# Pairs inside two neighbouring field groups computed in one burst of 32x64 TensorE tiles instead of two bursts of 64x128 tiles

## The reference, cut to what matters

```
z[b, (i,j)] = sum_e sum_f  e[b,i,e] * W[(i,j),e,f] * e[b,j,f]      # 780 pairs
h = concat(z, dense_ctx)                # 780 + 16
h = relu(h @ W_top1 + b_top1)           # 512
h = relu(h @ W_top2 + b_top2)           # 256
y = h @ W_top3                          # 1
```

## Time and profile before

| | us |
|---|---|
| median of 3 runs (range) | 751.01 (750.84 to 751.55) |
| the profiled execution: its time | 747.58 |
| its span | 745.8 |
| PE busy (share) | 689.6 (92%) |
| DVE busy | 546.2 (73%) |
| POOL busy | 446.0 (60%) |
| ACT busy | 67.2 (9%) |

### The profile page before, as it was taken

The page is one execution under the profiler, slowest core; times in us unless marked ns, Lnnn a source line. Parts: engine busy times, 40 slices in busy tenths (PEclk is TensorE's granted clock), DMA queues, the critical chain, the costliest instruction groups (busy, mean ns, idle before and its releaser), DMA issues.

```text
span 745.8 us, 13215 instructions
## 1 busy us (share of the span) xinstructions
PE 689.6 (92%) x5752; PEld 199.9 (27%) x5752; DVE 546.2 (73%) x518; ACT 67.2 (9%) x104; POOL 446.0 (60%) x452
## 2 busy tenths in 40 slices
PE   0779999989999999999899999999999999999998
PEld 0322233322222223232222222222322222222222
DVE  3858999978865668698766667869886667868900
ACT  4000000000000000101000000010010000010002
POOL 6777777777777777777777777777777300000000
PEclk9999999998999999999989999999999999999999
DMA  7730000030000000000300000000000000000000
GB/s 277 278 99 14 14 14 12 15 98 13 16 14 15 15 14 14 14 13 14 98 15 15 15 14 15 13 15 12 14 15 15 8 1 1 1 1 1 1 3 1
DMA packets 18081, 23.02 MB, mean 31 GB/s; under 512 B 8356, under 2 KB 16292, under 8 KB 17256
## 3 DMA queue, kind: packets, MB, share of 16 engines
q0 software_dynamic: 14336, 7.37, 5.7%
q1 hardware_dynamic: 2680, 12.78, 4.5%
q10 hardware_dynamic: 1008, 2.04, 0.8%
HBM read 22.09 MB, written 0.06 MB: 30 GB/s over the span
## 4 chain that ended last, share of the span: by engine, by line
PE 73%; DVE 14%; issue 6%; DMA 3%; ACT 2%; DVEq 0%; ACTq 0%
PE t_ps L510 21%; PE z_ps L522 20%; PE x_ps L541 11%; DVE prod L438 10%; PE x_ps L465 6%; PE t_ps L499 5%; DVE one_hot L425 3%; PE t_ps L541 3%; PE x_ps L554 3%; DMA hot_sb<-hot_ids 3%; PE x_ps L481 2%; ACT e_t L368 1%; PE x_ps L565 1%; PE t_ps L554 1%; DMA z_sb<-hot_tables 1%
## 5 line engine op out<-in xcount | busy, mean ns | idle before, releaser
L438 DVE TENSOR_TENSOR prod<-t_ps,e_t 128x1024 f32<-128x1024 f32 x400 | 468.3, 1218 | 134.0 <-PE t_ps L510 99.9
L331 POOL DMA_INDIRECT rows<-tbl,idx x448 | 445.8, 995 | 140.3 <-issue 135.9
L510 PE MATMUL t_ps<-e_t,w_sb 32*128 32x512 f32 x1440 | 227.8, 642 | 9.3 <-DVE prod L438 9.3
L522 PE MATMUL z_ps<-prod,select 128*32 128x512 f32 x1600 | 218.5, 603 | 1.1 <-DVE prod L438 0.7
L510 PEld LDWEIGHTS t_ps<-e_t,w_sb 32*128 32x128 f32 x1440 | 71.3, 184 | 164.8 <-DVE prod L438 96.6
L465 PE MATMUL x_ps<-one_hot,tables 128*32 128x512 bf16 x1272 | 86.5, 386 | 28.4 <-DVE one_hot L425 25.6
L425 DVE TENSOR_SCALAR one_hot<-hot_sb,row_number 128x2048 bf16<-128x2048 f16 (+1 forms) x112 | 78.4, 733 | 17.4 <-DMA hot_sb<-hot_ids 14.8
L541 PE MATMUL x_ps<-z_sb,w_sb 128*32 128x512 f32 x672 | 89.2, 613 | 2.0 <-ACT e_t L368 2.0
L522 PEld LDWEIGHTS z_ps<-prod,select 128*32 128x32 f32 x1600 | 46.4, 110 | 101.9 <-issue 70.1
L465 PEld LDWEIGHTS x_ps<-one_hot,tables 128*32 128x32 bf16 x1272 | 29.4, 97 | 100.9 <-issue 49.3
L499 PE MATMUL t_ps<-e_t,w_sb 64*128 64x512 f32 x160 | 46.4, 656 | 4.7 <-DVE prod L438 4.7
(11 more groups left out here) (18 smaller groups left out, 46.4 us busy)
## 6 DMA issues: line engine op xcount, KB each, us to landing
rows<-tbl,idx POOLq DMA_INDIRECT x448, 2.3
hot_sb<-hot_ids SPq DMA_DIRECT2D x4, 1536.0 KB, 6.5
w_sb<-w_lay SPq DMA_DIRECT2D x1, 1792.0 KB
z_sb<-hot_tables ACTq DMA_DIRECT2D x2, 640.0 KB, 6.0
w_sb<-w_lay SPq DMA_DIRECT2D x1, 1216.0 KB
w_sb<-w_lay SPq DMA_DIRECT2D x1, 960.0 KB, 10.6
w_sb<-w_lay SPq DMA_DIRECT2D x1, 704.0 KB, 8.8
w_sb<-w_lay SPq DMA_DIRECT2D x1, 640.0 KB, 6.2
```

The source lines that it names most:

```text
L331: pool.indirect_dma_start(out=rows[:, slot, t, E * f:E * f + E], out_offset=None, in_=tables[PER * c + f], in_offset=bass.IndirectOffsetOn ...
L438: nc.vector.tensor_tensor(prod[:, u % PROD_SLOTS, :, :], t_ps[:, at:at + 2, :], e_t[:, e_slot(k, c), :].unsqueeze(1).broadcast_to([P, 2, NB]),
L510: mm = nc.tensor.matmul(t_ps[:, at + r % 2, :], w_sb[part, b, :], e_t[part, e_slot(k, g), :], start=True, stop=True)
L522: mm = nc.tensor.matmul(z_ps[E * q:E * q + E, :], select[:, E - PER - PER * s:2 * E - PER - PER * s], prod[:, u % PROD_SLOTS, q % 2, :], s ...
```

## The change

The ten bursts (c, c) become five: (0,0), (2,2), (4,4), (6,6), (8,8), each of which holds the inner pairs of the groups c and c+1. Such a burst has eight matmuls of 32 rows by 64 columns, two for each 32-row strip, and fills four banks, two units, as the other bursts do. The 6 pairs of a group are spread over two row strips by two column halves. For that some column halves need the embeddings in another order (`FOLD`), so SP makes a re-ordered ("folded") copy of every group: three SBUF-to-SBUF DMAs for each (`FOLD_COPIES`), into a ring of four more slots of `e_t`. SP issues those of a pair of groups at the first burst of the odd group's column. TensorE and DVE wait for them before the inner burst; DVE's second operand there is the pair (slot, folded slot) instead of the slot repeated. The inner burst stands at the end of the odd group's column, (0,0) fourth. The number of units (100), batches (50) and reductions stays. The plan of `between` is written anew for 50 bursts. The ring `z_sb` has 10 slots instead of 12.

```diff
-BURSTS = [(g, c) for c in range(GROUPS) for g in range(c + 1)]
-BURST_UNITS = [1 if g == c else 2 for g, c in BURSTS]
+BURSTS = [(0, 1), (0, 2), (1, 2), (0, 0)]
+for _c in range(3, GROUPS):
+    BURSTS += [(_g, _c) for _g in range(_c)] + [(_c - 1, _c - 1)] * (_c % 2)
+UNITS = 2 * len(BURSTS)
-Z_RING = 12
+Z_RING = 10
-DIAGONAL = [[(0, 1), (1, 2), (0, 3)], [(2, 0), (3, 1), (2, 3)]]
+INNER = [{0: [(0, 1), (0, 2), (0, 3)], 1: [(1, 2), (1, 3), (2, 3)]},
+         {2: [(2, 0), (2, 1), (2, 3)], 3: [(3, 0), (3, 1), (0, 1)]}]
+FOLD = [[3, 2, 2, 3], [0, 1, 1, 0]]
+FOLD_COPIES = [[(0, 3, 1), (1, 2, 1), (2, 2, 2)], [(0, 0, 2), (2, 1, 1), (3, 0, 1)]]
+FOLD_RING = 4
...
-    plan = [(layer1_pieces(k - 1, 0), 0, 6), ([("turn", k, 4), ("turn", k, 5)], 7, 7),
-            (layer1_pieces(k - 1, 1), 7, 12), (layer1_pieces(k - 1, 2), 13, 18), ([("turn", k, 6)], 18, 18),
-            (layer1_pieces(k - 1, 3), 19, 24), ([("turn", k, 7)], 25, 25), ("hot", 0, 25, 29),
-            (layer2_pieces(k - 1, 0), 30, 32), ([("turn", k, 8)], 33, 33), (layer2_pieces(k - 1, 1), 33, 35),
-            ("hot", 1, 36, 42), ([("turn", k, 9)], 42, 42), (layer3_pieces(k - 1), 43, 44), ("hot", 2, 45, 52),
-            ([("turn", k + 1, c) for c in EARLY_TURNS], 53, 53)]
+    plan = [(layer1_pieces(k - 1, 0), 0, 5), ([("turn", k, 4)], 6, 6),
+            (layer1_pieces(k - 1, 1), 7, 10), ([("turn", k, 5)], 10, 10), (layer1_pieces(k - 1, 2), 11, 15),
+            ([("turn", k, 6)], 16, 16), (layer1_pieces(k - 1, 3), 17, 21), ([("turn", k, 7)], 22, 22),
+            ("hot", 0, 22, 26), (layer2_pieces(k - 1, 0), 27, 29), ([("turn", k, 8)], 30, 30),
+            (layer2_pieces(k - 1, 1), 30, 32), ("hot", 1, 33, 38), ([("turn", k, 9)], 38, 38),
+            (layer3_pieces(k - 1), 39, 40), ("hot", 2, 41, 47), ([("turn", k + 1, c) for c in EARLY_TURNS], 48, 48)]
...
+                elif kind == "gen" and BURSTS[step[2]][0] == 0 and BURSTS[step[2]][1] % 2:
+                    for c in (BURSTS[step[2]][1] - 1, BURSTS[step[2]][1]):
+                        sp.wait_ge(x_taken, use_no["e", k, c] + 1)
+                        if item(k, c) >= FOLD_RING:
+                            old_k, old_c = divmod(item(k, c) - FOLD_RING, GROUPS)
+                            sp.wait_ge(mult_done, first_unit(old_k, inner_at(old_c)) + 2)
+                        for to, source, count in FOLD_COPIES[c % 2]:
+                            sp.dma_start(e_t[E * to:E * (to + count), fold_slot(k, c), :],
+                                         e_t[E * source:E * (source + count), e_slot(k, c), :],
+                                         ).then_inc(folded[item(k, c) % FOLD_RING], 16)
...
+                        if g == c:
+                            near, far = e_slot(k, c + half), fold_slot(k, c + half)
+                            by = e_t[:, near:far + 1:far - near, :]
+                        else:
+                            by = e_t[:, e_slot(k, c), :].unsqueeze(1).broadcast_to([P, 2, NB])
...
                 if g == c:
-                    for half in range(2):
-                        part = slice(P // 2 * half, P // 2 * half + P // 2)
-                        mm = nc.tensor.matmul(t_ps[:, at + half, :], w_sb[part, b, :], e_t[part, e_slot(k, g), :],
-                                              start=True, stop=True)
+                    for of in (c, c + 1):
+                        pe.wait_ge(folded[item(k, of) % FOLD_RING], folds_of(k, of))
...
+                    else:
+                        near, far = e_slot(k, c + r // 2), fold_slot(k, c + r // 2)
+                        for side in range(2):
+                            source = far if (r, side) in ((1, 0), (3, 1)) else near
+                            cols = slice(P // 2 * side, P // 2 * side + P // 2)
+                            mm = nc.tensor.matmul(t_ps[cols, at + r % 2, :], w_sb[part, b, cols], e_t[part, source, :],
+                                                  start=True, stop=True)
```

More of the change, by code:

```diff
@@ L92, in between @@
     if k == 0:
-        turns = {c: block_of(0, c) - 2 for c in range(HOT_GROUPS + 1, GROUPS)}
+        turns = {c: begin_of(c) - 2 for c in range(HOT_GROUPS + 1, GROUPS)}
         for c, b in turns.items():
@@ L240, in tower_kernel @@
         table_cols = PER * E
-        assert 2 * max(blocks) * table_cols + sum(blocks) * table_cols <= Z_RING * NB
+        assert (max(blocks) + sum(blocks)) * table_cols <= Z_RING * NB
         tables_raw = z_flat[:, 0:all_blocks * table_cols].rearrange("p (v f) -> p v f", f=table_cols)
@@ L268, in tower_kernel @@
         gen_done = sem("gen_done")
+        folded = [sem(f"folded{n}") for n in range(FOLD_RING)]
         mult_done = sem("mult_done")
@@ L287, in _ @@
             for n, (first, last) in enumerate(W_PIECES):
-                a, b = block_of(0, first), block_of(0, last)
+                a, b = begin_of(first), begin_of(last)
                 sp.dma_start(w_sb[:, a:b, :], w_lay[:, a:b, :]).then_inc(w_loaded[n], 16)
@@ L430, in _ @@
                     g, c = BURSTS[b]
-                    if BURST_START[b] == 0 or BURSTS[b - 1][1] != c:
+                    if g == c:
+                        for of in (c, c + 1):
+                            dve.wait_ge(folded[item(k, of) % FOLD_RING], folds_of(k, of))
+                    elif g == 0:
                         dve.wait_ge(x_taken, use_no["e", k, c] + 1)
-                    for u in range(first_unit(k, b), first_unit(k, b) + BURST_UNITS[b]):
+                    for half in range(2):
+                        u = first_unit(k, b) + half
                         dve.wait_ge(gen_done, u + 1)
@@ L503, in gen @@
-                for r in range(PER):
-                    if r == 2:
-                        mm.then_inc(gen_done, 1)
-                        if u + 1 >= T_SLOTS:
-                            pe.wait_ge(mult_done, u + 1 - T_SLOTS + 1)
-                        at = 2 * ((u + 1) % T_SLOTS)
-                    part = slice(E * r, E * r + E)
-                    mm = nc.tensor.matmul(t_ps[:, at + r % 2, :], w_sb[part, b, :], e_t[part, e_slot(k, g), :],
-                                          start=True, stop=True)
@@ L632 @@
                 for slot in range(PER):
-                    place(b, r, PER * g + r, PER * c + slot)
+                    place(b, r, PER * g + r, PER * c + slot, slot)
         else:
-            for tile, edges in enumerate(DIAGONAL):
-                for source, target in edges:
-                    place(b, tile, PER * c + source, PER * c + target)
+            for half in range(2):
+                for r, edges in INNER[half].items():
+                    for source, target in edges:
+                        slot = target if source == r else FOLD[half].index(target, 0 if half == 0 else 2)
+                        place(b, r, PER * (c + half) + source, PER * (c + half) + target, slot)
     pairs = w.shape[0]
```

62 lines of the change are left out of this document (33 added, 29 removed).

## The result

The kernel after takes 717.85 us, median of 4 runs (717.5 to 718.62); the kernel before takes 750.92 (750.14 to 751.55) beside it. The ratio is 0.9561 [0.9545, 0.9578]. The gain is 33 us, where I forecast 21.7 and a range that ended at 723. The sign was right, and so was the price of the new burst. The size was not: a part of the change that I had not priced gave more than a sixth of the gain.

The account below looks back on a forecast made before the run. TensorE was taken to bind beside layers, VectorE in bare bursts, both near their limit beside look-ups; 10.2 + 3.2 + 0.9 + 0.9 + 1.4 + 0.9 + 5.3 - 1.1 = 21.7 us off 751.0 gave 729.3, range 723 to 734 (0.68).

Parts of the forecast that it names:

- The new burst: Inner-pair burst on TensorE: 1.07 us, in a range of 1.01 to 1.15 if its eight tiles run together.
- The rival that column halves go in turn: Column halves of a strip run one after the other, 1.9 us a burst: 744.5 us in all; chance 0.08.
- the slower case: Splitting tiles both ways serialises them further, 3.6 us a burst: about 780 us, slower than before; chance 0.04.
- VectorE's operand: Two slots in place of one repeated, in 40 of 400 products: the same 1218 ns a product.
- Turn 7: Chunk 0: needs the 80th gather, there at about 110.5, so only 1.6 us can be gained up to there.
- layers, turns and look-ups keep their number: TensorE's other work: only the inner pairs' matmuls change, so moved turns and pieces entered the sum at nothing.
- first 36 products, chunks 1 to 3: Columns up to 5, beside layer 1: six steps become three, 3.4 us a chunk, 10.2 us in three.
- next 28: Columns 6 and 7 of chunks 1 to 3: gains from bursts (6,6) and (7,7), 3.4 us.
- last 36: Columns 8 and 9 of chunks 1 to 3: gains from bursts (8,8) and (9,9), 3.9 us.
- chunk 0, from the span's start: Chunk 0, which has no layers: 5.3 us gained, capped by the gathers up to the turn of group 7.
- parity: Reductions in odd columns now wait for the product just ahead: 0.045 us for each of 25 bare bursts, 1.1 us lost.
- the copies free: 120 more DMAs on SP's queue cost nothing, at 0.34 us an issue; they might push turn 7 a microsecond or two.

Follow-up runs that it names:

- experiments 2 and 3: Kernel before with the turns of groups 4 and 5 split apart, 742.27 us; kernel after with them put back together in one step, 724.13 us.
- experiment 1: The kernel before, unchanged, profiled a second time: 748.04 us in one execution, beside a median of 750.18.
- experiment 9: Kernel after with no other user of the shared bank x_ps in the steps of turns 5, 7, 8 and 9: 707.97 us.
- Experiment 8: Kernel after with every reduction one batch later, so none waits for the product just ahead: 716.70 us.
- experiment 5: Kernel after without its 120 folded copies, inner bursts reading the plain embeddings (inner products then differ from the reference): 717.45 us.
- experiment 4: Kernel after with each matmul of the inner bursts issued twice in a row into the same bank: 735.41 us.
- experiment 6: Kernel after with SP waiting for the next chunk's hot ids to land before issuing the copies of groups 0 and 1: 717.91 us.

## Why the prediction came out as it did

**What was right.** The new burst: 1.05 us measured, 1.07 taken, and eight tiles split both ways run together. The rival that column halves go in turn (1.9 us a burst; I wrote 744.5 us, the sum gives 744.3) is refuted, and so is the slower case. TensorE does not wait for copies, VectorE's operand costs 1218 ns, the tail is 35.07 us long (710.72 to 745.80 in before is 35.08). Turn 7 waits for its gather, 1.28 us.

By the rule of the Trainium skill (TensorE: Matmul & The Clock Gate, Part 3, "What overlaps and what doesn't"), that a load overlaps running matmuls only in another row group, the burst would have been the 1.9 us case; for this form the trace does not agree, with 1.05. From the 62 ns a matmul that the Trainium skill (same page, Part 2, "Step-by-step") gives for a hardware decoder that is off I had made an estimate of some 1.17 us; the 1.05 don't bear that out, and how the decoder is set here no run shows.

**The step that failed** is the sentence "layers, turns and look-ups keep their number", with "Only the matmuls of the inner pairs change" behind it. The number is kept, and I let that stand for the cost: the re-placed turns and pieces are in the sum at nothing. The diff rewrote the plan, and the cost of such a step depends on its neighbours: two users of one bank behind the same burst add a hand-over of 0.68 us idle each, with changes of TensorE's tile mode between (0.1 us each, 0.98 against 0.88 in the earlier trace rows). That pair was in the trace of before, and in the diff. It is worth 5.6 us in three chunks by the traces (experiments 2 and 3). In the profiled execution of before the clock also fell behind it in chunk 1, which cost 1.6 there; but experiment 1 spends as much time at the lower level without that fall, and the new kernel more (mean clock 0.983), so I don't count the 1.6 as owed to the pair. With the pair put back the new kernel takes 724.13 us, which is inside the range, and 26.1 under the kernel before beside it: the pair explains why the range was left, and not the whole of the surplus.

**The sum, term by term,** by the stretches above. Pieces of layers that moved between stretches are set back by 0.88 each.

| | forecast | measured |
|---|---|---|
| first 36 products, chunks 1 to 3 | 10.2 | 7.4 + 5.7 + 5.7 = 18.9 |
| next 28 | 3.4 | 1.8 + 1.4 + 2.0 = 5.3 |
| last 36 | 3.9 | 0.5 + 0.9 + 1.2 = 2.6 |
| chunk 0, from the span's start | 5.3 | 3.0 |
| parity | -1.1 | inside the rows above |
| sum | 21.7 | 29.9 |

The measured sums are taken from hundredths and rounded after.

The first row less 5.6 and 1.6 is 11.7, against 10.2: 0.5 a chunk more than the steps I counted, and I have no experiment for it. In the second row the new plan changed neighbours as well; experiment 9 shows that such placement moves 0.7 to 1.8 us in this stretch, so I don't put the surplus down to the burst. In the last row the look-ups gave less than half a step back: there the two engines alternate, and a shorter step of one is partly a wait for the other. Experiment 8 got 1.2 us out of chunk 2's.

**Chunk 0** was over-sized by 1.7 us (5.3 less 0.6 of parity, against 3.0). It was capped by the gathers up to turn 7, as predicted, but cut there it is short on both sides. Turn 7 stands at 111.51 instead of 114.35. Of these 2.84 us two products are 2.26, so 0.6 were gained, where I had 1.6: I expected the last gather at 110.5, by GpSimd's times in before, and in this execution GpSimd began its 84th instruction, the 80th gather, some 1.1 us later:

```profile
0.00:109.10 109.10, 80.79 (x84) 0.95 0.43 132
```

At 109.0 it had begun 83 (before: 84 at 108.0). The copies are not shown to be the cause: without them (experiment 5) that gather began between 109.3 and 109.4.

Behind turn 7 I had 3.7 less 0.4 of parity, and 2.5 were gained. I had called the copies free, and there they are not. They sit behind the hot ids on one queue and made that load land 7.3 us after issue instead of 6.5, and VectorE waited 17.8 us for it in three loads instead of 14.8: 1.1 more ahead of chunk 0, where turn 7's own wait covers it, 0.6 in chunk 0's look-ups and 1.3 in chunk 1's. Each copy also took SP 0.67 us to issue, where I had taken 0.34.

**Parity.** Eight bare bursts of column 9 in chunk 3 (products 82 to 98, the last eight of its nine) take 18.47 us after and 18.10 before, 0.046 a burst, where I took 0.045. The size is right.

**What stays open.** Where the 3.4 us between the old kernel's profiled execution and its median lie. The median of the new kernel is only 0.2 from its profiled execution, so the median gains 3.2 us more than the traces; the mean clock speaks for the lower level (experiment 1), but no trace of a slower execution shows the place.

With 29.9 instead of 33, and less the 5.6 and the 1.6 of chunk 1's clock, 22.7 remain against my 21.7. That this is so near is in part luck. With parity set in its place the first 36 products gave 1.5 more than I priced and the next 28 gave 1.9 more, the last 36 gave 0.8 less and chunk 0 gave 1.7 less. The outcome under 723 had a chance of 0.05 in the prediction, and no mechanism was named for it.

## What to carry to other kernels

When a change rewrites a schedule, price the moved steps too: list, for each single-buffered bank, who uses it before and after each place, and count a hand-over for every two users with nothing between them. In this kernel moving a few entries of the plan (experiment 9, 8.0 to 9.9 us) was worth more than a third of what the new burst form was (about 23). And where a stage is capped by a late arrival, removing a wait ahead of it gains nothing until the arrival's user is moved as well.

## What the runs showed of the hardware

- Sixteen matmul instructions for eight 32x64 tiles of fp32, 512 columns, take 1.05 us from start to next start; a second round of the same adds 0.90 (experiment 4). A 64-column weight load is 129 ns by its mean, between 110 (32 columns) and 185 (128).
- A stall of TensorE can cost more than itself. In chunk 0, at turn 7, a wait of 2.87 us for the gather went with 6.8 us at the lower level of the clock (experiment 5) and one of 2.26 with 3.4 (experiment 6); behind one of 1.28 the clock stayed up (new kernel). In chunk 1 of the kernel before two waits of 0.68 us were followed by the lower level in one execution and not in another.
- SBUF-to-SBUF copies queued behind a 1.5 MB load of ids made it land later, 7.3 us by the median; without them it is 6.5 (before and experiment 5), with those of groups 0 and 1 issued behind its landing 6.7 (experiment 6). SP spends about 0.67 us on each of them (here time of the group, from 41.91, twelve issues):

```profile
41.91 8.07 SPq L340 DMA_DIRECT2D e_t<-e_t  x12
```

- One chip took 1184.96 us for the kernel before. On it TensorE's mean clock was 0.82 (0.98 elsewhere). In the trace of experiment 9's kernel there VectorE stood idle ahead of the one-hots for 202.8 us, in 13 waits of up to 32.8 us for an event that the profile does not name. The text on record of experiment 9's second run calls this the hot ids; the rows don't say so, and why the chip was slow stays open:

```profile
L458 DVE TENSOR_SCALAR one_hot<-hot_sb,row_number 128x2048 bf16<-128x2048 f16 (+1 forms) x112 | 78.0, 726 | 226.8 <-remote 202.8
...
104.53 0.76 DVE L458 TENSOR_SCALAR one_hot<-hot_sb,row_number 128x2048 bf16<-128x2048 f16 x1 [32.84 <-remote]
```
